# A graph network on one Trainium2 core: edge numbers corrected in four batches, and the preparation of the first two tiles placed inside the ranking

## The reference

```python
h = relu(layernorm(x))
x = x + L0(h)   # x@Wself.T + segment_sum(edge_weight * h[src], dst)@Wneigh.T, rows scaled to length 1
x = x + L1(h)   # two GCN convolutions: h@W, scaled by 1/sqrt(degree), summed over edges
x = x + L2(h)   # two hops of a degree-normalised weighted sum, then a product
x = x + L3(h)   # twice: 8 products per node by edge type, relu(xt[type, src]), summed by dst
```

## Time and profile before

| | |
|---|---|
| runs, us | 2903.17, 2909.96, 2911.70 (median 2909.96) |
| profiled execution, us | 2913.77 |
| its span, us | 2911.9 |
| TensorE busy | 2514.4 (86%), 12757 matmuls |
| TensorE weight loads | 1931.3 (66%) |
| VectorE busy | 1252.7 (43%), 2708 instructions |
| ScalarE busy | 581.2 (20%) |
| GpSimd busy | 824.9 (28%) |
| mean granted TensorE clock | 0.943 of full |

### The profile page before, as it was taken

The page is one execution under the profiler, slowest core; times in us unless marked ns, Lnnn a source line. Parts: engine busy times, 40 slices in busy tenths (PEclk is TensorE's granted clock), DMA queues, the critical chain, the costliest instruction groups (busy, mean ns, idle before and its releaser), DMA issues.

```text
span 2911.9 us, 33540 instructions
## 1 busy us (share of the span) xinstructions
PE 2514.4 (86%) x12757; PEld 1931.3 (66%) x12758; DVE 1252.7 (43%) x2708; ACT 581.2 (20%) x1742; POOL 824.9 (28%) x867
## 2 busy tenths in 40 slices
PE   6699999999979999999999998689898876666665
PEld 4488888888846678888777775456565545445554
DVE  7778888777556641111333333233343322222121
ACT  1155555555500320000111112011111110000000
POOL 2000000000000000000000000777777747777776
PEclk9799999999989999999999999899999987888888
DMA  2022222222246444444344443454454533333333
GB/s 75 1 99 90 102 85 102 86 102 85 102 155 230 170 147 147 158 148 147 123 145 140 148 148 105 134 155 146 152 155 147 160 121 111 110 109 109 109 111 96
DMA packets 144213, 361.50 MB, mean 124 GB/s; under 512 B 21408, under 2 KB 85006, under 8 KB 144042
## 3 DMA queue, kind: packets, MB, share of 16 engines
q1 hardware_dynamic: 45940, 194.06, 18.8%
q0 software_dynamic: 39936, 109.11, 13.0%
q10 hardware_dynamic: 58166, 56.07, 5.6%
HBM read 242.08 MB, written 117.07 MB: 123 GB/s over the span
## 4 chain that ended last, share of the span: by engine, by line
PE 57%; POOL 21%; DVE 9%; issue 9%; DMA 2%; ACT 2%; DVEq 0%; SPq 0%; POOLq 0%; ACTq 0%
PE agg L944 26%; POOL gathered L670 21%; PE y L764 10%; PE agg L844 6%; PE agg L1026 4%; PE y L805 4%; PE prod L757 3%; DVE gathered L1473 2%; DMA gathered<-table_rel,idx_rel 1%; ACT gathered L1131 1%; PE agg L833 1%; PE y L808 1%; DVE y_sb L1440 1%; PE turn_ps L742 1%; DVE slot_hot L1450 1%
## 5 line engine op out<-in xcount | busy, mean ns | idle before, releaser
L670 POOL DMA_INDIRECT gathered<-table_rel,idx_rel x832 | 805.7, 968 | 2063.5 <-DMA table_rel<-t_sb 1810.7
L1026 PE MATMUL agg<-gathered,stream 128*128 128x256 f32 x2400 | 626.6, 421 | 267.1 <-DMA gathered<-table_rel,idx_rel 243.4
L1026 PEld LDWEIGHTS agg<-gathered,stream 128*128 128x128 f32 x2400 | 495.5, 211 | 403.4 <-issue 205.0
L944 PE MATMUL agg<-t_sb,stream 128*128 128x256 f32 (+1 forms) x1875 | 380.5, 365 | 8.4 <-DMA stream<-counts_dense 8.4
L944 PE MATMUL agg<-gathered,stream 128*128 128x256 f32 (+1 forms) x1875 | 379.4, 361 | 0.0
L944 PEld LDWEIGHTS agg<-t_sb,stream 128*128 128x128 f32 (+1 forms) x1875 | 301.2, 161 | 83.7 <-issue 11.4
L944 PEld LDWEIGHTS agg<-gathered,stream 128*128 128x128 f32 (+1 forms) x1875 | 298.6, 159 | 71.8 <-issue 0.3
L844 PE MATMUL agg<-h_sb,stream 128*128 128x257 f32 x1250 | 336.6, 394 | 0.0
L1072 ACT COPY turned<-turn_ps 128x256 f32<-128x256 f32 (+2 forms) x100 | 39.9, 399 | 1141.6 <-PE turn_ps L742 1141.6
L805 PE MATMUL y<-gathered,relw 128*128 128x128 f32 x1300 | 237.9, 291 | 24.2 <-ACT t_sb L1148 17.6
L805 PEld LDWEIGHTS y<-gathered,relw 128*128 128x128 f32 x1300 | 220.2, 193 | 50.5 <-ACT t_sb L1148 23.1
(11 more groups left out here) (188 smaller groups left out, 1980.2 us busy)
## 6 DMA issues: line engine op xcount, KB each, us to landing
table_rel<-y_sb ACTq DMA_DIRECT2D x176, 256.0 KB, 3.2
stream<-weights_dense SPq DMA_DIRECT2D x50, 832.0 KB, 4.3
stream<-counts_dense SPq DMA_DIRECT2D x50, 800.0 KB, 4.3
stream<-weights_dense SPq DMA_DIRECT2D x50, 768.0 KB, 4.2
weights_dense<-stream SPq DMA_DIRECT2D x25, 832.0 KB, 3.4
weights_dense<-stream SPq DMA_DIRECT2D x25, 768.0 KB, 3.2
gathered<-table_rel,idx_rel POOLq DMA_INDIRECT x832, 2.7
counts_dense<-t_sb SPq DMA_DIRECT2D x25, 416.0 KB, 4.1
```

The costliest lines, as they stand in the source:

```text
L670: pool.indirect_dma_start(gathered[:, slot * D:(slot + 1) * D], None, tables[n], bass.IndirectOffsetOnAxis(ap=idx_rel[:, c:c + 1], axis=0) ...
L944: mm = pe.matmul(sums(n, t)[:, 0:width], of[:, s * P:(s + 1) * P], table(n, s), start=s == 0, stop=n in ("hop1", "hop2") and s == TILES - ...
L1026: mm = pe.matmul(agg[t % 2][:, 0:D], rel_hot[:, hot % HOT_RING, c - first, :], gathered[:, slot * D:(slot + 1) * D], start=c == lo, stop=c ...
```

## The change

The ranking's loop no longer corrects the numbers in each iteration. The numbers of all chunks are kept (in a free part of `relw`), and the seven instructions (`fix`) run four times, behind iterations 2, 7, 11 and 12, on 96, 160, 128 and 32 columns. Other work is placed behind iterations of the loop on VectorE: counting descents (1), `values_of(0)` (3), `slots_of(0)` (4), the statistics (5, 7, 9), `values_of(1)` (6), `slots_of(1)` (8), `take_tile(0)` and the destination one-hots of half tile 0 (11). TensorE permutes tile 0 behind group 11 and tile 1 behind group 19, and turns the weights behind groups 14, 18 and 21; ScalarE's copies of them come each behind one of its three blocks of normalised rows. The source one-hots of half tile 0 stay behind the loop, since they overwrite what the corrections read, and TensorE's first build has a new wait for them. `index_relations` moves to the end of the first layer, ahead of the reduction L1542. The functions `norm_stats` to `sage_pieces` only change their place in the text.

```diff
--- before.py
+++ after.py
@@ -95,6 +95,9 @@
     GR = 16
     RANKED = CHUNKS // GR
     COLS = GR * TILES
+    WEIGHTS_AFTER = (14, 18, 21)
+    PERMUTE_AFTER = (11, 19)
+    FIXED_AFTER = {2: 0, 7: 3, 11: 8, 12: 12}
...
@@ -213,12 +216,11 @@
             "p (k c d) -> p k c d", c=HOT_WIDE, d=P)
         hot_src = t_sb[:, 0:CHUNKS * TILES // 2].bitcast(BF16).rearrange("p (c s) -> p c s", s=TILES)
         picked = stream[:, 0, 0:2 * COLS].rearrange("p (k n) -> p k n", k=2)
-        number = stream[:, 1, 0:2 * GR]
-        number_i = stream[:, 1, 32:32 + 2 * GR].bitcast(I32)
-        number_l = stream[:, 1, 64:64 + 2 * GR].bitcast(I32)
-        spill = stream[:, 1, 96:96 + 2 * GR]
+        number_i = stream[:, 1, 0:CHUNKS].bitcast(I32)
+        number_l = stream[:, 1, CHUNKS:2 * CHUNKS].bitcast(I32)
+        spill = stream[:, 1, 2 * CHUNKS:3 * CHUNKS]
         relw_flat = relw[:].rearrange("p k r d -> p (k r d)")
-        src_tile, dst_tile, spills, rest, fit = (relw_flat[:, k * CHUNKS:(k + 1) * CHUNKS] for k in range(5))
+        src_tile, dst_tile, spills, rest, fit, number = (relw_flat[:, k * CHUNKS:(k + 1) * CHUNKS] for k in range(6))
...
@@ -707,7 +709,26 @@
                                      )[:, b * P:(b + 1) * P], 0)
             count_ends(1)
 
-
+            def turn_weight(k):
...
+                mm.then_inc(s_wt, 1)
+
+            def permute(t):
+                lo, hi = window(t)
+                pe.wait_ge(slots_ready, t + 1)
...
+                mm.then_inc(permuted, 1)
 
             for g in range(RANKED):
                 pe.wait_ge(s_hot, g // 2 + 1)
@@ -724,16 +745,10 @@
                                    carry[:, (g - 1) % 2, :].unsqueeze(1).broadcast_to([P, GR + 1, TILES]),
                                    start=False, stop=True, skip_group_check=True)
                 mm.then_inc(s_ranked, 1)
-
-            pe.wait_ge(s_w, 16 * 8)
...
-                mm.then_inc(s_wt, 1)
+                if g in WEIGHTS_AFTER:
+                    turn_weight(WEIGHTS_AFTER.index(g))
+                if g in PERMUTE_AFTER:
+                    permute(PERMUTE_AFTER.index(g))
             pe.wait_ge(s_wtc, 3)
 
...
-            def permute(t):
-                lo, hi = window(t)
...
                     mm.then_inc(sum_ready, 1)
 
-            permute(0)
-            permute(1)
+            pe.wait_ge(s_hot, RANKED // 2 + 1)
             for i in range(2 * (TILES - 1) + 9):
                 left = [((i - 1) // 2, s) for s in range(*PARTS[(i - 1) % 2])] if 1 <= i <= HALVES else []
                 if i < HALVES:
...
@@ -1060,7 +1063,7 @@
                 for t in range(lo, hi):
                     nc.scalar.activation(ht(t), xt(t), ACT.Relu, scale=rstd_all[:, t:t + 1],
                                          bias=shift_all[:, t:t + 1]).then_inc(s_scaled, 1)
-            for k, w in enumerate((wself_t, wneigh_t, hopw_t)):
+                w = (wself_t, wneigh_t, hopw_t)[k]
...
@@ -1314,116 +1317,25 @@
             copy_edges(0)
             count_ends(flat_f[:, 2 * F - 1:2 * F], 1)
 
-            for k in range(RANKED // 2):
-                if k + 1 < RANKED // 2:
...
-                prep(nc.vector.tensor_reduce(number, picked.rearrange("p k (c s) -> p (k c) s", s=TILES), AXX, ALU.add))
-                prep(nc.vector.tensor_copy(number_i, number))
-                prep(nc.vector.tensor_scalar(number_l, number_i, 2 * P - 1, None, ALU.bitwise_and))
-                prep(nc.vector.tensor_copy(number, number_l))
-                prep(nc.vector.scalar_tensor_tensor(spill, number, float(P), spills[:, chunks], ALU.is_ge, ALU.mult))
-                prep(nc.vector.tensor_tensor(bucket[:, chunks], src_tile[:, chunks], spill, ALU.subtract))
-                prep(nc.vector.tensor_scalar(spill, number, float(P), -float(P), ALU.is_ge, ALU.mult))
-                prep(nc.vector.scalar_tensor_tensor(slot1[:, chunks], number, 1.0, spill, ALU.add, ALU.add))
+            def fix(chunks):
+                prep(nc.vector.tensor_copy(number_i[:, chunks], number[:, chunks]))
+                prep(nc.vector.tensor_scalar(number_l[:, chunks], number_i[:, chunks], 2 * P - 1, None, ALU.bitwise_and))
+                prep(nc.vector.tensor_copy(number[:, chunks], number_l[:, chunks]))
+                prep(nc.vector.scalar_tensor_tensor(spill[:, chunks], number[:, chunks], float(P), spills[:, chunks],
+                                                    ALU.is_ge, ALU.mult))
+                prep(nc.vector.tensor_tensor(bucket[:, chunks], src_tile[:, chunks], spill[:, chunks], ALU.subtract))
+                prep(nc.vector.tensor_scalar(spill[:, chunks], number[:, chunks], float(P), -float(P),
+                                             ALU.is_ge, ALU.mult))
+                prep(nc.vector.scalar_tensor_tensor(slot1[:, chunks], number[:, chunks], 1.0, spill[:, chunks],
+                                                    ALU.add, ALU.add))
                 dve.sem_inc(s_pos, 1)
-                if k == 4:
-                    dve.wait_ge(s_x, 16 * len(LOADED))
-                if 4 <= k < 4 + len(NORMED):
-                    stats(k - 4)
-                    scales(k - 4)
-            dve.wait_ge(s_pos, RANKED // 2)
-
-            def index_relations():
-                nc.vector.scalar_tensor_tensor(idx_rel[:], edges[:, :, 3], float(NPAD), edges[:, :, 0],
-                                               ALU.mult, ALU.add).then_inc(s_idx, 1)
-
-            index_relations()
-
-
-            prep(nc.vector.memset(drops[:], 0.0))
-            prep(nc.vector.tensor_tensor(drop[:, 0:F - 1], flat_f[:, F:2 * F - 1], flat_f[:, F + 1:2 * F], ALU.is_gt))
-            dve.wait_ge(s_next, 16 * 2)
-            prep(nc.vector.tensor_tensor(drop[:, F - 1:F], flat_i[:, 2 * F - 1:2 * F], row_next[:, 0:1], ALU.is_gt))
-            prep(nc.vector.tensor_reduce(drops[0:QP, 0:1], drop, AXX, ALU.add))
-            dve.wait_ge(s_wtc, 3)
-
...
+            def count_drops():
+                prep(nc.vector.memset(drops[:], 0.0))
+                prep(nc.vector.tensor_tensor(drop[:, 0:F - 1], flat_f[:, F:2 * F - 1], flat_f[:, F + 1:2 * F], ALU.is_gt))
+                dve.wait_ge(s_next, 16 * 2)
+                prep(nc.vector.tensor_tensor(drop[:, F - 1:F], flat_i[:, 2 * F - 1:2 * F], row_next[:, 0:1], ALU.is_gt))
+                prep(nc.vector.tensor_reduce(drops[0:QP, 0:1], drop, AXX, ALU.add))
...
                         dve.wait_ge(deg_done, h - 1)
-                    equal(src_hot[:, h % 2, 0:count, :], 0, slice(lo, hi))
+                    made = equal(src_hot[:, h % 2, 0:count, :], 0, slice(lo, hi))
                     if own:
-                        equal(src_hot[:, h % 2, count:count + 1, :], 0, slice(TILES, BCK))
+                        made = equal(src_hot[:, h % 2, count:count + 1, :], 0, slice(TILES, BCK))
+                    if h == 0:
+                        made.then_inc(s_hot, 1)
                 if what == "dst":
                     if own:
                         equal(pair_hot[:, h % 2, count:count + 1, 1, :], 1, slice(TILES, BCK))
                     equal(pair_hot[:, h % 2, 0:count, 1, :], 1, slice(lo, hi)).then_inc(cnt_ready, 1)
+
+            for k in range(RANKED // 2):
+                if k + 1 < RANKED // 2:
+                    onehots_of_tiles(k + 1)
+                chunks = slice(2 * k * GR, 2 * (k + 1) * GR)
+                for j in range(2):
+                    g = 2 * k + j
+                    dve.wait_ge(s_ranked, g + 1)
+                    nc.vector.tensor_copy(carry[:, g % 2, :], rank_ps[j][:, COLS:COLS + TILES]).then_inc(s_carry, 1)
+                    nc.vector.tensor_tensor(picked[:, j, :], rank_ps[j][:, 0:COLS],
+                                            hot_src[:, g * GR:(g + 1) * GR, :].rearrange("p c s -> p (c s)"), ALU.mult
+                                            ).then_inc(s_picked, 1)
+                dve.wait_ge(s_picked, 2 * k + 2)
+                prep(nc.vector.tensor_reduce(number[:, chunks], picked.rearrange("p k (c s) -> p (k c) s", s=TILES),
+                                             AXX, ALU.add))
+                if k in FIXED_AFTER:
+                    fix(slice(2 * FIXED_AFTER[k] * GR, 2 * (k + 1) * GR))
+                if k == 1:
+                    count_drops()
+                if k == 3:
+                    dve.wait_ge(s_fields, 1)
+                    dve.wait_ge(s_const, 12)
+                    values_of(0)
+                if k == 4:
+                    slots_of(0)
+                    dve.wait_ge(s_x, 16 * len(LOADED))
+                if k in (5, 7, 9):
+                    stats((k - 5) // 2)
+                    scales((k - 5) // 2)
+                if k == 6:
+                    values_of(1)
+                if k == 8:
+                    slots_of(1)
+                if k == 11:
+                    take_tile(0)
+                    onehots(0, "dst")
+            dve.wait_ge(s_pos, len(FIXED_AFTER))
+
+            def index_relations():
```

(69 more changed lines are left out.)

89 lines of the change are left out of this document (29 added, 60 removed).

## The result

The changed kernel takes 2891.3 us (median of 4 runs, 2889.1 to 2892.3) against 2910.8 (four runs, 2903.2 to 2911.8; the forecast was worked against the 2910.0 of three); the ratio is 0.9934, with a 95% interval from 0.9921 to 0.9947. The forecast was 2893, in a range of 2883 to 2902. The profiled execution has a span of 2890.5 us, 21.4 shorter than the earlier trace rows.

The account below looks back on a forecast made before the run. The prediction took VectorE to bound the ranking. An earlier first build saved 23.7 us, less 5.5 for clock falls and 0.9 for the index instruction: 17.3 off the 2910.0 median, predicted 2893 us, range 2883 to 2902.

Parts of the forecast that it names:

- The bound and the price of an iteration: Ranking loop: VectorE is the bound; an iteration costs the larger of TensorE's 5.07 us and VectorE's 3.89 plus extras.
- the price of the corrections: Ranking on VectorE: seven small instructions cost 1.65 us an iteration, 3.62 in iteration 0, 23.4 in all before the change.
- four batches, together: Ranking on VectorE: corrections on 96, 160, 128 and 32 columns cost 2.12, 2.58, 2.35 and 1.65, in all 8.7 us.
- iterations 10 and 11, full clock: Ranking: iteration 10 at TensorE's 5.07 us, iteration 11 at 3.89 plus 2.35, 0.88 and 2.0; forecast 14.2 together.
- last pick to first build: Behind the ranking: last reduce and batch 2.68 us, tile 0's source one-hots 2.01, hand-off 0.1; forecast 4.8.
- exposed clock falls: Ranking: TensorE's clock falls behind idle gaps, some four at 1.3 us, 5.5 taken between bounds 0 and about 9.
- index instruction at the layer's end: End of the first layer on VectorE, ahead of the reduction: nothing covers it, so 0.9 us is paid whole.
- the signs: Expected in the trace: first build near 120, last pick near 115, iteration 11 9 to 10 us, later span unchanged but 0.9.
- Rival (a): Ranking: TensorE's clock falls no more often than now or its price hides in VectorE's long iterations; 2887 us, chance 0.12.
- Rival (b): Ranking: the low clock stays throughout and TensorE becomes the bound, an iteration 9.7 us; the whole 2917 us, chance 0.02.
- Rival (c): First build: a late transfer or late normalised rows from ScalarE cost the whole gain; 2910 or 2911 us, chance 0.04.
- Rival (d): Correction batches: wide integer steps slower than the slope, 2.8 us more at twice it; 2896, within the forecast's 0.73 chance.

Follow-up runs that it names:

- Placement alone: The changed kernel with the seven corrections run again in every iteration on 32 columns, other moved work left in place: 2897.3 us, ratio 0.9962.
- batches alone: The kernel before with only the four wide correction batches, the other work not moved: 2894.0 us, ratio 0.9949.
- the six variants: Six edited kernels: corrections per iteration, batches only, filler matmuls, index instruction moved, statistics in VectorE's waits, and that with the rest spread; medians 2876.4 to 2897.3 us.
- the last kernel: The changed kernel with statistics in VectorE's waits and batches, slots, records, index instruction, one-hots and a permutation spread over other iterations: 2876.4 us, ratio 0.9896.
- the statistics in the waits: The changed kernel with the statistics' first step moved into VectorE's wait between an iteration's two groups: 2881.0 us, ratio 0.9906.
- matmuls in the gaps: The changed kernel with unread matmuls on TensorE ahead of its carry waits of groups 17 and 25: 2883.0 us, ratio 0.9911.

## Why the prediction was right

The bound and the price of an iteration held. "An iteration then costs the larger of 5.07 and 3.89 plus its extras" gave 7.62, 7.96 and 7.94 for iterations 3, 5 and 6, and they took 7.62, 7.95 and 7.94. Placement alone confirmed the price of the corrections on both sides of that sum, and batches alone the floor of TensorE (4.91 a full iteration; 5.07 was 0.16 too much). Iteration 1 the sum charged at 5.07 + 1.75, which is not the larger of the two but both, and gave no reason. It took 6.68, so both were paid: VectorE waited 1.62 us in it for TensorE, and the extra stands behind that wait.

| step | forecast, us | measured |
|---|---|---|
| four batches, together | 8.7 | about 8.05: 1.97, 2.30, 2.1 and 1.65 |
| iterations 10 and 11, full clock | 14.2 | 14.25 |
| last pick to first build | 4.8 | 4.89 |
| first build without falls | 116.3 | 115.1 (118.17 less 3.07) |
| exposed clock falls | 5.5, some four | 3.1, two: 0.79 in iteration 8, 1.47 in 9, 0.8 in 12 (second trace: 2.3) |
| index instruction at the layer's end | 0.9 | 0.83 |
| gain up to the first build | 18.2 | 21.8 |
| gain of the median | 17.3 | 19.5 |

The term that was mis-sized is the clock. Its 1.3 us a gap is a third of the 3.9 that followed the three gaps behind the blocks of statistics in the kernel before. In that kernel's second trace the gaps are 4.54, 3.72 and 4.21 us, the carry matmuls behind them took 1.79, 1.79 and 1.78 us instead of 0.99, and the granted clock was 0.50 over each of the three. Iterations 3 and 6 left TensorE idle for 2.5 and 2.4 us, and their falls didn't come; I took the middle of the bounds. The trace of before had one gap of that length, which the sum didn't use: in iteration 1 the carry matmul behind 2.43 us, and the counting behind it, were fast.

```profile
33.65 0.99 PE L723 MATMUL y<-carry,ident 128*128 128x425 f32 x2 [2.43 <-DVE carry L1324]
```

It would have spoken for a smaller term, but not proved it, since behind 2.43 us the clock did fall in the second trace of the changed kernel. The price of the clock differs from one execution of the same program to the next: 3.1 us in one trace and 2.3 in the other.

What is left, about 1.2 us, is the batches' 0.65 and 0.4 in iteration 0, where TensorE sped up sooner (the counting of group 1 took 2.16 us, in the kernel before 2.56). The batches took the 8.0 that the prediction gave as its lower end, but not by its reason: if only the three two-input operations of the seven grew, at 1.04 ns a column, they would take 7.5 us. The other four grow too, by about 0.5 ns a column (0.18 to 0.24 us for 128 columns more).

Of the signs, the last pick ended at 113.2 ("near 115"), and the wait ahead of the source one-hots was 0.22. Iteration 11 lasted 10.4 us and not 9 to 10, because iteration 10 took 3.9 for 5.1: VectorE met TensorE's floor one iteration later. From the first build to the end the span grew by 0.4 us, where 0.9 was forecast.

Rival (a), a cheaper clock, was half right: 2887 was its time, and two of the four falls didn't come. Rival (b), the slow clock through the ranking, didn't show in any of ten traces. In or behind each of the eleven longest gaps ahead of a carry matmul, 3.52 to 5.18 us, the clock fell, but it came back soon (in the second trace of the kernel before the carry matmuls took 1.79 us at 59.91 and 0.96 at 64.01, then 1.78 at 81.15, 1.53 at 85.96 and 0.97 at 88.98), and most gaps are shorter. A fall at every turn didn't come. Rival (c) is out: the shift was passed on to the end but for 0.4 us. Rival (d) is out, the wide integer step takes 0.24 us at 160 columns. (Its price of 2.8 us was too high: twice the slope adds another 2.1 to the sum.)

That the median was met within 2 us is in part luck. The first build came 3.6 us sooner than the sum had it, and the median's gain, 19.5, is smaller than the 21.4 between the profiled executions, within the spread of the runs. One part of that spread stays open. In the ten traces the first layer took 674.3 to 679.7 us and the rest 2086.2 to 2093.3, with the same instructions but for the index instruction. In the layer the granted clock goes with it (679.7 at 0.98 in its first 200 us, 676.6 at 1.00, for the same program). In the rest two repeats agreed within 0.6 us (2093.3 and 2092.8; 2092.6 and 2093.2), while the six variants had 2086.2 to 2093.2. Whether the time at which the stage starts, the place of the code or chance sets this wasn't tried. Of the 43.2 us between the spans of the kernel before and of the last kernel (2911.9 and 2868.7), 33.7 lie ahead of the first build (139.97 less 106.26). The other 9.5 are this open part, 2.4 in the first layer and 7.1 behind it; the index instruction stands at the end of the layer in neither of the two kernels.

## What to carry to other kernels

Where two engines pass work back and forth, write down each one's time for a round. Work that moves into such a loop is paid in full on the engine that bounds it, and free in the other's slack, in an unavoidable wait inside the round, or in a round where the other engine is the bound. So look for the hand-off's own wait (here 0.60 us in every round) before looking for idle rounds.

And sum an engine's floor over several rounds, since it can run ahead through the long ones, and what it does at the end of a round is met only in the next (a floor of 6.6 us charged to one round measured 5.21, and 0.96 came in the round behind).

## What the runs showed of the hardware

The fall of TensorE's granted clock from 1.00 to 0.50 behind idle time isn't a function of the gap's length alone. In the ranking a gap of 2.43 us had a fall right behind it in two traces and none in six others, one of 2.54 (2.53 in one) had a fall in one trace and none in five, and behind 3.29 us (batches alone, granted clock 1.00 from 70.61 to 74.00) none came. Behind 2.93 or 2.94 the carry matmul was slow, in whole or in part, in all four traces that have it (1.78 or 1.79 us in three, 1.37 in the statistics in the waits).

The fall need not meet the first matmul. Behind 3.48 and 3.52 us the carry matmul at the gap's end still took 0.99 us, and the counting behind it 3.06 and 2.96: the granted clock went to 0.50 some 1.1 to 1.3 us after TensorE had started again.

And its price depends on where it lands: in the carry matmul (1.78 instead of 0.99 us) VectorE waits for it (1.40 us instead of 0.60), in the counting beside VectorE's long work it cost nothing (2.94 instead of 1.63 us in iteration 7 of the changed kernel's second trace), and in a round bound by TensorE it was paid (matmuls in the gaps: the counting 2.81 us in iteration 10, iterations 10 and 11 longer by 1.7).
